# Routed results stored in table order and gathered by GpSimd, the table zeroed early, and four shared matmuls moved among the routed tiles

## The reference, cut to what matters

```python
shared_enc = _expert_stack(x, sW1, sb1, sW2, sb2).sum(0)      # 128 -> 512 -> 128, gelu
weights = softmax(x @ gW + gb)                                # 15 routed experts
topv, topi = top_k(weights, 3)
gated = (one_hot(topi, 15) * topv[..., None]).sum(-2)
router_out = _expert_stack(x, rW1, rb1, rW2, rb2)             # each 128 -> 256 -> 128, gelu
router_enc = einsum('ebtd,bte->btd', router_out, gated)
x = layernorm(shared_enc + router_enc + x)
```

## Time and profile before

| | us |
|---|---|
| Timed, median of 3 runs | 286.7 (285.6 to 286.87) |
| Span of the profiled execution | 319.6 |
| First tile turned by PE, in the profiled execution | 208.85 |
| Last result copied out by ACT | 312.01 |

### The profile page before, as it was taken

The page is one execution under the profiler, slowest core; times in us unless marked ns, Lnnn a source line. Parts: engine busy times, 40 slices in busy tenths (PEclk is TensorE's granted clock), DMA queues, the critical chain, the costliest instruction groups (busy, mean ns, idle before and its releaser), DMA issues.

```text
span 319.6 us, 7117 instructions
## 1 busy us (share of the span) xinstructions
PE 241.1 (75%) x2283; PEld 179.8 (56%) x2283; DVE 221.6 (69%) x630; ACT 192.2 (60%) x423; POOL 179.0 (56%) x166
## 2 busy tenths in 40 slices
PE   6989989877988767996761299688868867785970
PEld 3676868655535434452451156586857757674960
DVE  6777999989999998998520497043444434856875
ACT  4697997549976976754470350344554546563665
POOL 6132755330666738985677467135656566665752
PEclk9999999999997998998978589799999999999778
DMA  7672830124000002952211133123132263354462
GB/s 218 217 213 46 181 128 2 37 67 133 2 0 2 0 4 62 378 215 49 86 58 50 44 101 108 41 61 101 53 99 76 75 187 90 91 168 123 150 185 90
DMA packets 38597, 31.89 MB, mean 100 GB/s; under 512 B 12864, under 2 KB 31552, under 8 KB 38432
## 3 DMA queue, kind: packets, MB, share of 16 engines
q1 hardware_dynamic: 34608, 23.90, 26.6%
q0 software_dynamic: 3520, 7.27, 6.7%
q10 hardware_dynamic: 432, 0.27, 0.3%
HBM read 19.95 MB, written 11.47 MB: 98 GB/s over the span
## 4 chain that ended last, share of the span: by engine, by line
PE 44%; DVE 27%; issue 14%; ACT 4%; another core or an unknown queue 4%; POOL 4%; DMA 1%; DVEq 0%; SPq 0%; ACTq 0%
PE psum L994 12%; PE psum L985 9%; PE psum L783 5%; DVE prob_sums L1496 4%; PE psum L763 4%; DVE maxes L1490 3%; PE psum L977 2%; PE psum L568 2%; DVE prob_sums L1410 2%; POOL x_srt L1986 2%; PE psum L585 1%; DMA xT<-x_t 1%; DVE turned_room L1421 1%; DVE maxes L1405 1%
## 5 line engine op out<-in xcount | busy, mean ns | idle before, releaser
L2047 POOL DMA_INDIRECT y_tok<-k_heads,y_rows x62 | 62.7, 1012 | 50.8 <-ACT k_heads L1327 34.4
L1319 ACT ACTIVATE k_heads<-psum,k_heads 128x128 f32<-128x128 f32 x124 | 38.7, 365 | 38.5 <-PE psum L985 33.6
L1986 POOL DMA_INDIRECT x_srt<-v_blocks,slot x48 | 48.0, 1000 | 21.3 <-issue 17.2
L994 PE MATMUL psum<-k_heads 128*128 128x128 f32 x248 | 42.4, 295 | 18.0 <-issue 12.1
L1823 DVE COPY k_heads<-psum 128x128 f32<-128x128 f32 x62 | 17.8, 289 | 48.9 <-PE psum L977 32.7
L994 PEld LDWEIGHTS psum<-k_heads 128*128 128x128 f32 x248 | 34.2, 200 | 21.9 <-issue 15.2
L985 PE MATMUL psum<-k_heads 128*128 128x128 f32 x248 | 40.6, 288 | 5.2 <-DVE k_heads L1823 4.2
L1963 POOL TENSOR_TENSOR k_heads<-k_heads,inv_sums 128x1024 f32<-128x1024 f32 x14 | 27.1, 1939 | 24.0 <-DVE inv_sums L1503 23.9
L985 PEld LDWEIGHTS psum<-k_heads 128*128 128x128 f32 x248 | 33.8, 198 | 8.5 <-DVE k_heads L1823 7.4
L1951 POOL TENSOR_TENSOR probs<-probs,inv_sums 128x512 f32<-128x512 f32 x16 | 16.8, 1050 | 28.9 <-DVE inv_sums L1415 28.7
L1327 ACT ACTIVATE k_heads<-psum,k_heads 128x128 f32<-128x128 f32 x62 | 22.9, 370 | 11.3 <-PE psum L994 9.1
(11 more groups left out here) (191 smaller groups left out, 530.1 us busy)
## 6 DMA issues: line engine op xcount, KB each, us to landing
expert_w<-e_w SPq DMA_DIRECT2D x1, 4369.0 KB
k_heads<-x_srt SPq DMA_DIRECT2D x62, 65.0 KB
q_heads<-y_tok SPq DMA_DIRECT2D x8, 256.0 KB
x_srt<-pad SPq DMA_DIRECT2D x16, 65.0 KB
xT<-x_t SPq DMA_DIRECT2D x4, 256.0 KB, 5.1
ctxT_k<-ctx_k SPq DMA_DIRECT2D x2, 512.0 KB, 5.5
v_scr<-v_rows SPq DMA_DIRECT2D x4, 256.0 KB, 2.8
ctxT_v<-ctx_v SPq DMA_DIRECT2D x2, 512.0 KB, 5.0
```

The source lines that it names most:

```text
L994: mm = pe.matmul(bank[6 + t % 2][:, 0:E], h_tile[:, t % 2, a, :], tile_weights(t)[:, FE + E * a:FE + E * a + E], start=(a == 0), stop=(a = ...
L1319: ins = act.activation(h_tile[:, t % 2, a, :], bank[2 + t % 2][:, P * a:P * a + P], ACT.Gelu, bias=tile_weights(t)[:, EW - 2 + a:EW - 1 + a])
L1986: pool.indirect_dma_start(out=x_srt, out_offset=bass.IndirectOffsetOnAxis(ap=slot[:, n:n + 1], axis=0), in_=payloads[:, g, k, :], in_offse ...
L2047: pool.indirect_dma_start(out=y_tok, out_offset=bass.IndirectOffsetOnAxis(ap=y_rows[:, t:t + 1].bitcast(mybir.dt.uint32), axis=0), in_=y_t ...
```

## The change

- One table `rows_srt` of 34,816 rows of 128 numbers takes the place of `x_srt` and `y_tok`. The gate and the result's row number are no longer in it; gates stay in SBUF (`gate_cols`). The scatter's row is x alone, so ACT's copies of x for the second and third choice (`payload`) are gone.
- The whole table, 17.8 MB, is filled with zeros by eight transfers that ACT issues from a zeroed piece of SBUF (`rows_cleared`), four between the exps of the first attention and four ahead of those of the second. POOL's first scatter and SP's load of `expert_w` wait for all of them. SP's 16 transfers of empty rows are gone.
- The result of a tile is stored by SP at the rows of the table from which the tile was loaded (`y_stored`), and no longer scattered by POOL. The load of tile t + 8 now waits until tile t + 1 is turned.
- POOL, done with its scatters, reads 16 counts and then gathers, for each quarter as its tiles are stored, 12 row groups by the slot numbers it already has (48 indirect transfers into `routed_y`).
- DVE applies the gate as it adds (`added`, 12 operations of 128x128 for each quarter instead of 3 of 128x512). Quarters 0 and 1 are added in the loop (t = 42 and 57), quarters 2 and 3 behind it; the last quarter goes row group by row group (`added_last`). The roots, the norm and the stores of the first quarters stand behind the loop.
- `shared_in` of the last quarter becomes four single matmuls among the tiles (i = 13, 14, 16, 17), with its gelus on ACT behind them; `shared_out` of that quarter moves to t = 21, 24, 27 and 30.

The core of the diff:

```diff
+ROWS = (NE + 1) * ROOM
-            sp.wait_ge(s_filled, 16 * (NE + 1))
+            def y_stored(t, rows):
+                sp.wait_ge(s_y_tile, t + 1)
+                if t >= NY:
+                    sp.wait_ge(s_y_stored[t % NY], 16 * (t // NY))
+                sp.dma_start(rows_srt[bass.ds(rows[t // 4][t % 4], P), :], y_tile[:, t % NB, :]).then_inc(s_y_stored[t % NY], 16)
...
             for t in range(NT):
...
+                if t + NB < NT:
+                    if t % 4 == 0:
+                        rows[(t + NB) // 4] = row_of(t + NB)
+                    sp.wait_ge(s_tile_turned, t + 1)
+                    x_loaded(t + NB, rows)
+                y_stored(t, rows)
...
-            shared_in(6)
-            shared_in(7)
...
+                if i in SHARED_IN_TILES:
+                    shared_in_late(SHARED_IN_TILES.index(i))
...
+            def rows_cleared(first, count):
+                act.wait_ge(s_zeros, 1)
+                for i in range(first, first + count):
+                    n = ROWS * E // P // Z
+                    part = rows_srt.rearrange("(p r) e -> p (r e)", p=P).rearrange("p (n z) -> p n z", z=Z)
+                    part = part[:, i * n // FILLS:(i + 1) * n // FILLS, :]
+                    act.dma_start(part, zeros.unsqueeze(1).broadcast_to([P, part.shape[1], Z])).then_inc(s_filled, 16)
...
-            payload(0)
...
-                    act.activation(y_tile[:, t % NB, :], bank[6 + t % 2][:, 0:E], ACT.Copy,
-                                   scale=x_tile[:, t % NB, E:E + 1]).then_inc(s_y_tile, 1)
+                    act.copy(y_tile[:, t % NB, :], bank[6 + t % 2][:, 0:E]).then_inc(s_y_tile, 1)
...
-                dve.tensor_tensor(acc[:, 4 * c:4 * c + 4, :], acc[:, 4 * c:4 * c + 4, :],
-                                  routed_y[k][:, 4 * c:4 * c + 4, :], ALU.add).then_inc(s_y_sum, 1)
+                for g in range(4 * c, 4 * c + 4):
+                    ins = dve.scalar_tensor_tensor(out=acc[:, g, :], in0=routed_y[k][:, g, :], scalar=gate_cols[:, g, k:k + 1],
+                                                   in1=acc[:, g, :], op0=ALU.mult, op1=ALU.add)
+                ins.then_inc(s_y_sum, 1)
...
-            for t in range(NT):
-                pool.wait_ge(s_y_tile, t + 1)
-                pool.wait_ge(s_y_rows, t // 4 + 1)
-                pool.indirect_dma_start(out=y_tok, out_offset=bass.IndirectOffsetOnAxis(
-                    ap=y_rows[:, t:t + 1].bitcast(mybir.dt.uint32), axis=0),
-                    in_=y_tile[:, t % NB, :], in_offset=None).then_inc(s_y_scattered[t % NB], 16)
+            for c in range(NC):
+                for k in range(NY):
+                    pool.wait_ge(s_y_stored[k], landed[c][k])
+                pool.sem_inc(s_y_through, 1)
+                for n in range(4 * TOPK * c, 4 * TOPK * (c + 1)):
+                    g, k = n // TOPK, n % TOPK
+                    pool.indirect_dma_start(out=routed_y[k][:, g, :], out_offset=None, in_=rows_srt,
+                                            in_offset=bass.IndirectOffsetOnAxis(ap=slot[:, n:n + 1], axis=0)
+                                            ).then_inc(s_y_got[c] if c < NC - 1 else s_y_last[g % 4], 16)
```

## The result

| | before | after |
|---|---|---|
| Timed, median | 286.15 us (285.28 to 286.87, 4 runs) | 318.4 us (318.12 to 320.43, 4 runs) |
| Ratio | | 1.1175, 95% interval 1.1103 to 1.1246 |
| Span of the profiled execution | 319.6 us (283.0 in a second one, below) | 316.6 us |
| First scatter of x on POOL | 118.4 us | 137.5 us |
| First tile turned | 208.85 us | 205.67 us |

What follows compares the result with a forecast made beforehand. The prediction took POOL's scatter to limit the loop at 1.33 us per tile, with PE and DVE leading the whole chain. It summed 286.7 + 4.9 (loop and end) - 1.0 (ahead of the loop) = 290.6 us, range 283.5 to 301.

Steps and rivals of the forecast that it cites:

- the fill: Ahead of the loop: four issues on ACT at each of two places, 0.54 us each, +3.5 us, bounds 0 and 4.4.
- The reading of the profile's extra: Of 32.9 us not in timed runs, 14.4 are two waits without known releaser; the other 18.5 lie in the loop.
- the fill holds ACT: Rival, chance 0.12: pieces beyond 2176 must move before ACT goes on, 11.8 us per place, 22.8 instead of 3.5; 309.9 us.
- The loop: From first tile turned to the end: 97.2 us instead of 92.3, +4.9, since the last quarters' gathers come late.
- The rival of cheaper gathers: Rival, chance 0.16: POOL's gathers cost 0.96 us each instead of 1.26, loop term -2.0; 283.7 us.
- the time at which tile 44 is stored: In the loop: result at 56.5 us after the first turn, stored at 59.3, when quarter 2's gathers can start.
- the pace: In the loop: 1.08 for SP + 0.06 shared matmuls + 0.07 waits = 1.21 us per tile, bounds 1.08 and 1.33.
- the store's landing: In the loop: tile 44's store takes 0.5 us to issue and 2.3 us to land.
- Ahead of the loop: Before the first tile: -3.6 for `shared_in`, -0.9 for POOL's first scatter, +3.5 for the fill, sum -1.0 us.
- -3.6 us for `shared_in`: Ahead of the loop: the last quarter's `shared_in` leaves PE's row, which runs without a gap into the first tile; bound 0.
- -0.9 for POOL's first scatter: Ahead of the loop: its 1.16 us wait, read as gates and copies of x, mostly goes; bound 0.

Runs made afterwards that it cites:

- the second trace: The kernel before, unchanged, profiled once more: run 284.8 us, span 283.0 us.
- undone: The changed kernel with its eight fill transfers issued by SP instead of ACT: 299.42 us, 1.0559 of before.
- alone: The kernel before with only the eight fill transfers from ACT added, into a table that nothing reads: 304.76 us, 1.0745 of before.
- the run that it was built on: The changed kernel with the fill on SP and the last quarter's shared matmuls at the end of the loop: 297.5 us, 1.0451 of before.
- the two later runs: Fill on SP with the last quarter's shared matmuls at the loop's end, 297.5 us; the same with six stores ahead of SP's wait, 295.91 us.

## Why the prediction was wrong, by its own steps

The forecast was 290.6 us and its range 283.5 to 301; 318.4 were measured. Two steps failed: the fill, whose issues were priced as if they could not hold ACT, and the time at which the gathers can start in the loop. Without the held ACT the run is at 299.42, inside the range.

**The reading of the profile's extra** (14.4 us ahead of the loop, 18.5 in it) came near for the loop: from the first tile turned to the end are 283.0 - 190.1 = 92.9 us in the second trace, and 92.3 were worked out. Ahead of the loop the extra was 18.8 (208.85 - 190.09). The waits of the earlier trace rows were its largest part, as was read: in the second trace DVE waits 1.79 us at the place of the 11.03, and not at all at that of the 3.42.

**The fill** failed by its term. It was priced at 3.5 us with issues of 0.54 each, from SP's small loads; it cost 19.0 (undone) and 20.2 (alone). This was the rival "the fill holds ACT", given 0.12 and 22.8 us, with 2176 pieces as the point from which it decides. The traces bear that out: two transfers, 1024 + 1152 = 2176 pieces, go through in 1.0 us, and from the third on ACT pays, 10.8 us for the third and fourth at the first place and 9.4 at the second, where the rival had 11.8. (Its sum of 309.9 us has the forecast's loop in it and is still 8.5 short.) Where between 2176 and the next 1024 pieces it begins no run shows. The row that decided was in the prediction: one load of 2176 pieces at 0.37 us says nothing on twice as many, and a bound from it belonged into the sum, not behind it. The Trainium skill's "Perfetto Trace Analysis", in its section on the DMA instruction by HWDGE, has an issue last until all descriptors are generated; the 5.07 and 5.68 us of the third and fourth issue fit that, though no trace here shows the generating itself. What the forecast also missed is how far ACT's loss goes: 8.9 and 8.3 us, 17.1 in all, come out at POOL's first scatter in full, 137.45 against 118.78. DVE's two waits, 8.26 and 7.65 us, pass them on, and the chain that ended last runs through the held issues of both places.

**The loop** was predicted at +4.9 us; without the held ACT it is (297.1 - 185.4) - 92.9 = +18.8. The mechanism stood in the prediction: quarter 2's gathers wait for tile 44, 24 of them follow at 1.26 us (measured 1.25 undisturbed, 1.29 on average), the last quarter's without a pause, and the end comes 8.9 us behind the start of the last one (measured 297.1 - 287.75 = 9.35). The rival of cheaper gathers, with 0.96 from one to the next, is out by these rows. One number was far off, the time at which tile 44 is stored: 59.3 us after the first turn was predicted, and the gathers began at 258.12 - 185.36 = 72.8. The first turn, and the stores of tiles 0 and 44, in the run with the fill on SP:

```profile
185.36 0.64 PE L966 MATMUL psum<-consts,k_heads 128*128 128x128 f32 x2
...
198.21 0.38 SPq L461 DMA_DIRECT2D rows_srt<-k_heads  x1
...
254.90 0.90 SPq L461 DMA_DIRECT2D rows_srt<-k_heads  x1
```

Of these 13.5 us:
- 9.5 are the start. The prediction let tile 0 be stored as soon as it is finished, 3.3 us after the first turn. SP's order has the wait for the last scatters of x ahead of its first store, and the last of those ends on POOL at 196: the first store is at 198.21, 12.85 us after the first turn. The edit that added the stores to SP's queue was priced by its 0.54 us, but not by what stands ahead of it in that queue. The run with six stores ahead of the wait recovered part of it: tile 44 is stored 62.9 us after the first turn there, instead of 65.8 in the run that it was built on.
- 3.5 are the pace, 1.29 us per tile between the stores of tiles 0 and 44 (198.21 and 254.90) instead of 1.21. Only the 3.6 us of `shared_in` had been spread over the tiles; `shared_out` of that quarter lies among these 45 tiles too, and both are 9.4 us of PE there. With all of it behind these tiles the pace is 1.20 (199.56 to 252.48). Part of that difference is the clock: tiles 8 to 10 took 5.8 us at the lower level in the one run, and only two tiles fell to it in the other. In the kernel before, `shared_out` in the loop should have cost nothing, since POOL's 1.26 us left PE time; that `shared_in` costs nothing there was measured (0.9999).
- 0.4 are the store's landing.

The window view of the run with the fill on SP shows PE full in that stretch, and its first 5.8 us at half the clock (the columns are those of the earlier trace rows):

```profile
199.60:205.40 5.80, 5.80 (x28) 5.80 (x29) 1.98 (x6) 2.39 (x8) 0.00 (x0) 0.50 0.43 118
...
199.50:216.00 16.50, 16.41 (x98) 14.31 (x99) 6.46 (x20) 9.19 (x32) 0.00 (x0) 0.82 0.39 110
216.00:230.00 14.00, 14.00 (x115) 12.98 (x114) 6.63 (x20) 8.80 (x32) 5.65 (x6) 1.00 0.41 112
230.00:245.00 15.00, 15.00 (x137) 15.00 (x136) 9.84 (x29) 10.20 (x40) 11.34 (x13) 1.00 0.59 156
```

**Ahead of the loop**, -3.6 us for `shared_in` and -0.9 for POOL's first scatter were counted as won. POOL's wait did fall from 1.15 to 0.19 us. PE did come earlier: 185.36 instead of 190.09 in the run with the fill on SP. But tile 8 was turned at 199.58 instead of 200.29, because its load waits for the last scatter of x, and PE stood for 6.35 us where it had stood for 2.29:

```profile
199.58 0.47 PE L966 MATMUL psum<-consts,k_heads 128*128 128x128 f32 x1 [6.35 <-DMA k_heads<-rows_srt]
```

The step that failed is that PE's row, "which runs without a gap into the first tile", sets when the loop ends, so that 3.6 us off it are won. That was so in the first trace, where the extra between the router and the first tile had made PE late; in the second PE waits 0.84 us for the first load, and tile 8's load and the scatters of results wait for POOL's scatters of x. Moved alone, `shared_in` brought 0.9999.

**Where the 32 us are**, then: 19 from the fill on ACT's queue (17.6 by the ratios), and 14 between the traces of 283.0 and 297.1. Read on POOL, these 14 are: in the kernel before it goes from x to results with no pause, and its last needed transfer starts at 266.29, 16.7 us ahead of the end. In the changed one it is idle for 26.8 and 4.4 us and does 48 gathers instead of the 54 scatters, the last at 287.75, 9.3 us ahead of the end: 21.5 later, 7.4 given back. The wish behind the change, POOL out of the loop, came true, and that is its price: the gathers can only start when tiles are stored, while the scatters had filled that time. This part is an account of two traces. No run took the wait in front of the first gather away, and the two that shortened it, by 0.5 and 2.4 us, came with a time 1.9 and 3.5 us shorter (3.1 and 3.5 by the ratios), with DVE's work behind the loop as the next limit.

What stays open: the run with the fill on SP has its first scatter at 118.78, and 117.83 less the wait that fell away would be 116.9. No single wait in the trace accounts for these 2 us. They may be the fill's bytes, or no more than the spread of single executions: the two later runs with the same order up to there have it at 119.41 and 120.08.

## What to carry to other kernels

A transfer is priced by its bytes only while the queue takes it; count the pieces that are in flight, and give long fills to an engine that nobody waits for, or spread them. Work taken out of a busy engine's row is only a gain if what replaces it can start as early: here scatters that ran as results came were replaced by gathers that wait for a whole quarter. And where an instruction is added to a queue, look at the wait that stands ahead of it there; before any of this, compare the profiled execution's span with the timed runs, and profile again when they differ by a tenth.

## What the runs showed of the hardware

- Issues hold their engine when earlier transfers are still in flight: 0.40, 0.61, 5.07 and 5.68 us for four transfers of 1024 or 1152 pieces of 2 KB, one behind the other, and 0.4 to 0.6 for each of two when the pair before had been issued 14 us earlier.
- Another engine's issues were held as well: while ACT's fill was in flight, eight issues on SP took 16.04 us instead of 4.57, and in the changed kernel itself the eight that reload the first layer norm's output took 10.42 instead of 3.94.
- Gathers and scatters of 128 rows of 512 bytes cost POOL the same where nothing delayed them: 0.94 to 0.96 us each, 1.25 to 1.26 from one to the next.
- An execution under the profiler can be 36 us longer than another one of the same kernel (319.6 and 283.0). The extra was not spread evenly: 0.6 us up to POOL's first scatter at 118, 18.2 from there to the first tile, 17.9 behind it.
- After PE had waited 6.35 us its groups of four matmuls took 1.06 us instead of 0.61 for 6 groups; the granted clock in these 5.8 us was 0.50, the lower of the two levels (1.2 GHz), 0.82 on average over the 16.5 us from there, and 1.00 in the next stretch.
